# Four transformer layers on one core: layer 2's first maxima from on-chip parts, its router later, and its experts prepared inside the last attention group

## The reference, cut to what matters

```python
# layer 2, x: (1024, 256); xn = layernorm(x); T = 1024, 16 heads, hd = 16
q, k, v = split(xn @ w_qkv.T)
scores = einsum('bhqd,bhkd->bhqk', q, k) * hd ** -0.5      # causal
attn = softmax(scores); attention = (attn @ v) @ w_out.T

scores = xn @ gate_w.T                                      # 8 experts
ew, ei = top_k(scores, 2); ew = softmax(ew)
x1 = silu(einsum('td,ehd->teh', xn, w_gate))
x3 = einsum('td,ehd->teh', xn, w_up)
expert_out = einsum('teh,edh->ted', x1 * x3, w_down)
routed = sum over e of comb[t, e] * expert_out[t, e]        # comb: ew at the chosen experts
shared = (silu(xn @ sh_gate.T) * (xn @ sh_up.T)) @ sh_down.T
x = x + attention + routed + sigmoid(xn @ se_gate_w.T) * shared
```

## Time and profile before

| what | us |
|---|---|
| median of 3 runs (919.77 to 921.51) | 920.62 |
| the profiled execution, as a run | 929.83 |
| its span, first to last instruction | 928.1 |
| TensorE busy in it | 840.9 |
| VectorE, ScalarE, GpSimd busy | 562.2, 386.6, 236.5 |

### The profile page before, as it was taken

One profiled execution on the slowest core, in us unless ns is written; L12 is line 12 of the kernel. 1 busy time (PEld: TensorE's weight loads), 2 busy tenths in 40 slices (PEclk: granted clock), 3 DMA queues, 4 the chain that ended last, 5 costly groups with the idle time before them and its releaser, 6 DMA issues.

```text
span 928.1 us, 12052 instructions
## 1 busy us (share of the span) xinstructions
PE 840.9 (91%) x4835; PEld 497.8 (54%) x4835; DVE 562.2 (61%) x999; ACT 386.6 (42%) x477; POOL 236.5 (25%) x211
## 2 busy tenths in 40 slices
PE   8998999999899999996899998679999889989997
PEld 3554453445354435444478794523333258888776
DVE  3878658774876678216443553577778326964552
ACT  2641345346444645563523402115556763510240
POOL 4641322421142114513321101400111137710110
PEclk8979999999999999998889997769999989999999
DMA  6464069315731850204000004949000061000001
GB/s 187 77 198 124 23 147 162 90 70 86 119 81 68 140 142 1 77 1 152 8 1 1 1 3 152 126 104 121 2 1 1 1 237 47 0 1 1 0 1 46
DMA packets 35584, 64.99 MB, mean 70 GB/s; under 512 B 6164, under 2 KB 14908, under 8 KB 35460
## 3 DMA queue, kind: packets, MB, share of 16 engines
q1 hardware_dynamic: 34952, 64.08, 29.7%
q10 hardware_dynamic: 576, 0.13, 0.1%
HBM read 44.35 MB, written 16.29 MB: 65 GB/s over the span
## 4 chain that ended last, share of the span: by engine, by line
PE 65%; DVE 19%; ACT 5%; DMA 4%; SPq 3%; issue 2%; POOL 2%; ACTq 0%; DVEq 0%; POOLq 0%
PE psD L1808 11%; PE psO L1946 11%; PE psA L1808 10%; PE psD L1891 9%; PE psA L1909 8%; DVE mx L1384 8%; PE psO L1808 7%; PE psA L1908 3%; SPq L604 3%; PE psD L1893 2%; ACT Pr L1054 2%; DVE hid_low L1704 1%; DMA Ks<-in_c_ones4b 1%; PE psD L1960 1%; POOL Pr L905 1%
## 5 line engine op out<-in xcount | busy, mean ns | idle before, releaser
L1384 DVE TENSOR_REDUCE mx<-psD 128x1 f32<-128x512 f32 (+3 forms) x418 | 258.4, 657 | 89.1 <-PE psD L1893 63.7
L1054 ACT ACTIVATE Pr<-psA 128x1024 f32<-128x1024 f32 (+3 forms) x192 | 161.8, 866 | 161.7 <-PE psA L1909 161.3
L905 POOL TENSOR_SCALAR_AFFINE_SELECT Pr<-Pr 128x512 f32<-128x512 f32 x96 | 61.1, 637 | 385.5 <-ACT Pr L1054 309.8
L1059 ACT ACTIVATE Pr<-psA 128x1024 f32<-128x1024 f32 (+3 forms) x96 | 63.6, 703 | 60.6 <-PE psA L1909 60.3
L1946 PE MATMUL psO<-Pr,Vh 128*32 128x512 f32 (+3 forms) x768 | 80.8, 500 | 3.1 <-POOL Pr L905 2.5
L1908 PE MATMUL psA<-Qr,Kr 128*128 128x512 f32 (+3 forms) x192 | 75.0, 404 | 0.7 <-ACT xnT L1014 0.7
L1893 PE MATMUL psD<-maskq,identb 128*128 128x128 bf16 x350 | 70.8, 227 | 0.0
L1909 PE MATMUL psA<-Qr,Kr 113*128 113x512 f32 (+3 forms) x192 | 65.8, 349 | 0.0
L1891 PE MATMUL psD<-Kg,Qs 96*128 96x512 bf16 (+3 forms) x192 | 54.9, 334 | 7.8 <-DVE mx L1384 4.9
L1891 PE MATMUL psD<-Kr,Qr 80*128 80x512 bf16 (+3 forms) x166 | 50.6, 347 | 7.0 <-DVE mx L1384 6.1
L1891 PE MATMUL psD<-Ks,Qs 96*128 96x512 bf16 (+3 forms) x166 | 51.5, 354 | 4.7 <-DVE mx L1384 3.7
(11 more groups left out here) (420 smaller groups left out, 1684.3 us busy)
## 6 DMA issues: line engine op xcount, KB each, us to landing
Qr<-d_qr SPq DMA_DIRECT2D x18, 512.0 KB, 11.6
d_qr<-WB SPq DMA_DIRECT2D x9, 512.0 KB, 3.5
Pr<-d_cb SPq DMA_DIRECT2D x8, 512.0 KB, 7.0
Qs<-d_gq SPq DMA_DIRECT2D x24, 128.0 KB, 4.1
Qs<-d_q SPq DMA_DIRECT2D x24, 128.0 KB
Ks<-d_k SPq DMA_DIRECT2D x24, 128.0 KB
Qr<-d_qn SPq DMA_DIRECT2D x18, 128.0 KB, 7.2
Kr<-d_kn SPq DMA_DIRECT2D x18, 128.0 KB, 7.9
```

Of the source, the lines that this page charges most:

```text
L905: pool.affine_select(out=block_, in_=block_, pattern=[[0, GH], [1, P]], compare_op=ALU.is_ge, fill=0.0, base=0, channel_multiplier=-1).the ...
L1054: act.activation(place[:, h, q0:T], src[:, q0:T], ACT.Exp, scale=score_scale(i)).then_inc(a_drained, 1)
L1059: act.activation(place[:, h:h + 2, q0:T], src[:, :, q0 - HALF:HALF], ACT.Exp, scale=score_scale(i)).then_inc(a_drained, 1)
L1384: dve.tensor_reduce(mx[:, j, part, h0:h0 + nh], src, AX, ALU.max).then_inc(d_drained, 1)
```

## The change

It touches layer 2 alone, in three places.

*The first maxima.* ScalarE now copies each query and key unit twice: the bf16 high part and the fp32 value. VectorE makes four copies of k tile 0's high part, in each of which only the rows of one head are kept (`masked_keys`, with the 0/1 matrix `head`); group 8's maxima are then products of q tile 0's high part with a masked key over all 128 rows, with no stack. k tile 1's product and the values tiles are placed between these units. VectorE splits only u0; GpSimd splits u1, u2 and u3 (three steps each, the first being ScalarE's copy now). SyncE's order is: store u0, store u1, stack 8, store u2, stack 9, store u3, then stacks 10 and 11 (once the first four score units of group 8 are there) and `comb` behind them.

*The router.* Its products come behind (10, 0), the choice of experts at (10, 5), the weights and `magnitudes()` at (11, 1), the weights' transposes and copy at (11, 3). The sigmoid becomes an exponential, an addition and a reciprocal.

*The experts' preparation.* The cuts of the first three pieces (kt 0 to 2) and the high parts of `xnT` (kt 3 and 4) are made by ScalarE inside group 11, with the low parts on GpSimd and VectorE. Behind group 11 expert 0's first product comes at once; the output's transposes follow it, and the transposes of `xn` come before hidden unit 2.

```diff
-                if u < 2:
+                if u == 0:
                     sp.wait_ge(split_done, n)
                 else:
-                    sp.wait_ge(late_split_done, u - 1)
+                    sp.wait_ge(late_split_done, u)
                 load((d_q2, d_k2)[u % 2][:, tile_cols(u // 2), :].rearrange("s d t -> d s t"),
                      split_place(n)[1], split_stored[n % 3])
                 if u == 1:
                     sp.wait_ge(split_stored[0], 16 * 2)
                     sp.wait_ge(split_stored[1], 16 * 2)
                     load_stack(GROUPS[2][0])
+                if u == 2:
                     load_stack(GROUPS[2][1])
             sp.wait_ge(split_stored[0], 16 * 3)
             sp.wait_ge(split_stored[2], 16)
-            sp.wait_ge(a_drained, A["cT"])
-            load(d_cb, seT[:], comb_out)
+            sp.wait_ge(a_filled, A["v2"] + GH)
             load_stack(GROUPS[2][2])
             load_stack(GROUPS[2][3])
+            sp.wait_ge(a_drained, A["cT"])
+            load(d_cb, seT, comb_out)
...
+            for u in (1, 2, 3):
+                pool.wait_ge(a_drained, A["xnT2"] + u + 1)
+                for k in (1, 2, 3):
+                    split_step(3 + u, k, late_split_done)
...
+                    if i == LAST and kt in (1, 2, 3):
+                        piece_low(kt - 1)
...
+                        if (i, kt) == (LAST, 1):
+                            act.wait_ge(se_args, 1)
+                            act.activation(sig3[:], lr[:, 9, 0:3 * NT].rearrange("p (j s) -> p j s", s=3), ACT.Exp,
+                                           scale=-1.0).then_inc(se_ready, 1)
+                        if (i, kt) == (LAST, EXPERTS_KT):
+                            act.wait_ge(split_stored[0], 16 * 3)
+                            copy_units([seT])
...
+                        if i == LAST and kt < 3:
+                            cut_piece(kt)
+                        if i == LAST and 3 <= kt < 3 + DC:
+                            act.activation(x2_high[:, kt - 3, :], xnT[:, kt - 3, :], ACT.Copy).then_inc(x2_cut, 1)
...
-                copy_units([split_place(3 + u)[0]])
+                v, b = split_place(3 + u)
+                src = take()
+                act.activation(b[:, 0], src, ACT.Copy).then_inc(part0_cut, 1)
+                act.activation(v, src, ACT.Copy).then_inc(a_drained, 1)
...
+            act.activation(gam[:, 0:1], ln[:, 1, 0:1], ACT.Exp)
+            act.wait_ge(late_split_done, 3)
+            act.wait_ge(split_stored[0], 16 * 2)
             act.wait_ge(split_stored[1], 16 * 2)
             act.wait_ge(split_stored[2], 16)
             maxima_row(GROUPS[2][0])
...
+            split(3, A["xnT2"] + 1)
+            dve.wait_ge(part0_cut, 2)
+            dve.wait_ge(head_ready, 1)
+            for h in range(GH):
+                dve.tensor_scalar(masked_keys(h), split_place(4)[1][:, 0], head[:, h:h + 1], None,
+                                  ALU.mult).then_inc(keys_masked, 1)
...
+                    pe.wait_ge(keys_masked, GH)
+                    last_keys = None
+                    for k, (j, part, h0, nh, w) in enumerate(MAX_UNITS):
+                        maxima_unit(groups[0], j, h0, nh, w, part)
+                        if k == 3:
+                            last_keys = a_unit()
+                        if k in (3, 8):
+                            features(cols(w_qkv2, 3 * P, 4 * P), normed, halves=(k // 8,), dst=last_keys)
+                        if k >= 13 and k % 3 == 1 and k < 13 + 3 * NT:
+                            value_tile((k - 13) // 3)
+                    maxima_transpose(groups[0], GH)
                     arrived(groups[0])
...
+                        if (i, kt) == LOGITS_AT:
+                            logits = d_unit()
+                            for j in range(NT):
+                                op = product(logits[:, j * (E + 1):(j + 1) * (E + 1)],
+                                             [(xnT[:, k, tile_cols(j)], w_rt2[:, k, :]) for k in range(DC)])
+                            op.then_inc(d_filled, 1)
...
             for m in range(E + DC):
+                if m == 2:
+                    pe.wait_ge(d_drained, DU[f"o{LAST}"])
+                    transposed(xn)
                 pe.wait_ge(piece_split, m + 1)
                 features(weights2(m, 0), parts2, range(3 * DC))
+                if m == 0:
+                    output_transposes(LAST)
+                    pe.wait_ge(gsum_ready, 1)
+                    pe.matmul(d_unit()[:, 0:4], onesf[:], gam[:, 0:4], start=True, stop=True).then_inc(d_filled, 1)
```

More of the change, by code:

```diff
@@ L279, in build @@
         gam = sb("gam", [P, 12])
+        head = sb("head", [P, GH])
         Qr, Kr = over("Qs", "Qr", [P, 8 * T]), over("Ks", "Kr", [P, 8 * T])
@@ L484, in build @@
             + [("xnT1", 1), ("v1a", 1), ("xnT1b", 1), ("qk1", 1), ("v1", 1), ("xh", DC), ("s1", NT), ("gate1", FC)]
-            + [("xnT2", DC), ("qk2", 4), ("v2", 2), ("cT", 1)]
-            + [(f"att{i}", A_GROUP) for i in GROUPS[2]] + [("oT2", DC), ("gate2", E + DC)]
+            + [("xnT2", DC), ("qk2", 4), ("v2", 2)]
+            + [(f"att{i}", A_GROUP) for i in GROUPS[2][:-1]]
+            + [("first of the last", GH * EXPERTS_KT), ("cT", 1), (f"att{LAST}", A_GROUP - GH * EXPERTS_KT)]
+            + [("gate2 first", 2), ("oT2", DC), ("gate2", E + DC - 2)]
             + [("xnT3", DC), ("k3", DC), ("g3", DC), ("sig3", F3C)])
@@ L1477, in attention @@
                 if groups[0] > 0:
-                    magnitudes()
+                    for c in range(DC):
+                        dve.wait_ge(x2_cut, c + 1)
+                        dve.tensor_tensor(x2_low[:, c, :], xnT[:, c, :], x2_high[:, c, :], ALU.subtract).then_inc(x2_split, 1)
                     outputs(groups[-1])
@@ L2049, in attention, with value_tile @@
                     values_product(*behind, (0, 1))
-                    output_transposes(groups[-1])
+            value_place = [None]
+            def value_tile(j):
+                if j % 4 == 0:
+                    value_place[0] = a_unit()
+                op = product(value_place[0][:, (j % 4) * D:(j % 4 + 1) * D],
+                             [(xnT[:, k, tile_cols(j)], w_qkv2[:, k, 2 * D:3 * D]) for k in range(DC)])
+                if j % 4 == 3:
+                    op.then_inc(a_filled, 1)
             def down(u, terms):
```

149 lines of the change are left out of this document (75 added, 74 removed).

## The result

The changed kernel takes 916.77 us (median of 20 runs, 910.76 to 925.68) beside 922.58 us for the kernel before on the same chip (20 runs, 917.92 to 930.27). The ratio is 0.9929, with a 95% interval of 0.9909 to 0.9949: 6.5 us less, 4.7 to 8.4. The prediction was -9.4. By ratio the change is worth less than the two profiles suggest, and the experiments say why.

What follows compares the result with a forecast made beforehand. In layer 2's front nothing computes at the limit; a chain of stores, stack loads and maxima sets it. The terms -12.1 + 0.5 + 3.2 + 2.9 - 3.9 = -9.4 gave 911.2 us, with an 8-in-10 range of 905.5 to 918.5.

Steps and rivals of the forecast that it cites:

- Front, -12.1 and +0.5: Layer 2's front: group 9's first maxima unit at 612.7 instead of 624.8, -12.1; TensorE starting at the low clock, +0.5.
- the wait for stack 9 covers both: Layer 2's front: stack 9, there at 612.7, hides the maxima's end (599 to 604) and first score (602 to 608).
- TensorE waits 5 to 9 us for the last load of a stack just behind the first score: Sign expected in the front's profile after, with group 9's first unit at 612 to 614.
- Masked keys: Layer 2's front: VectorE makes four 128x1024 copies at 0.7 us each, 2.8 us in all, costing nothing behind stack 9's wait.
- Router, +3.2: Group 10, behind kt 0: the 16 small products add 3.2 us, from 2.5 if gaps take some.
- TensorE is nearly always busy in that group, so they are added: Group 10: the reason for counting the router products' 3.2 us in full.
- Last group, +2.9: Group 11: ScalarE gets 4.9 us of cuts, copies and exponential, partly hidden in gaps; +2.9 us, bounds 1.5 and 5.0.
- Experts, -3.9: Start of the experts: expert 0's product follows group 11 at once, 4.3 us come in between; -3.9 us, bounds -5.5 and -2.
- (a): Front: loads move at 353 GB/s or more, maxima set the front; -16.3 in all, 904.3 us; 7 in 100.
- (b): Maxima stage: TensorE's clock stays low, first unit at 622 to 627; -0.6 to +4.4, about 922.5 us; 8 in 100.
- (c): Group 11 and experts: port quarrel slows GpSimd and VectorE, ScalarE's 4.9 us come in full; -1.8, 918.8 us; 13 in 100.
- (d): Front: nothing moves because the new stage waits for something else as late as 624; +2.2 us; 2 in 100.

Runs made afterwards that it cites:

- the second measurement: The changed kernel, unedited, timed and profiled again beside three of its variants: 919.32 us, ratio 0.9966 to the kernel before.

## Why the prediction was right, and where it wasn't

The forecast of faster and the range (905.5 to 918.5) held with 916.77; the narrower 907.5 to 915.5, given 70 in 100, did not, and the second measurement, 919.32, is just outside both. The size was too large. Term by term, from the two profiles on the common clock:

- **Front, -12.1 and +0.5.** Group 9's first unit is at +52.0 instead of +62.9 (608.65 and 624.82, from 556.67 and 561.89), -10.9; up to group 8's `OT` another 0.6 is gained. -11.5 beside a forecast of -11.6. The size is right, but the step "the wait for stack 9 covers both" is wrong. What is late is the row of maxima, which the prediction took at its price in an empty queue and had in time at 602 to 608. The sign "TensorE waits 5 to 9 us for the last load of a stack just behind the first score" failed: the wait is 8.27 us and stands ahead of the score. That the two come out alike is luck. Both end with the queue's traffic, and this ended at 607.0 + 5.2 = 612.2 on the clock of before, where the prediction had stack 9. But the measured traffic has k1's store in it, behind the stack, and the sum had no time for that. The rate rises to a store's, 283 GB/s and more, at 605.0, so stack 9 itself was through near 605, some 2 us earlier than reckoned; the store and the row's late packets filled these 2 us. The prediction had said that it trusted this order least.
- **Masked keys.** 6.2 us for four, where 2.8 was taken. The one that ran without GpSimd took 0.48, less than the 0.7 for one; the others took 1.25 to 2.36 beside GpSimd's split, each ending just behind one of its steps. That is the quarrel of the two engines that the prediction read from the earlier trace rows, and its bounds had allowed for it. In this execution it cost nothing, since the wait for the queue covers it, as the prediction said of all of this stage; where the queue was quick (the row issued at 599.27, the traffic ended at 599.0) the maxima set the front, and these microseconds stand in it. The bound of 577 to 582 for the start of the maxima held (573.70 + 5.2 = 578.9).
- **Router, +3.2: the term that was mis-sized.** It measured +5.1. The products take 3.9 us of it, and the 1.2 left is the clock that falls to half behind them: in the one profile in which it didn't fall, nothing was left. The step "TensorE is nearly always busy in that group, so they are added" counted their length, 0.7 us short, and not the clock behind them. In other executions the same place costs 6.7 us, and up to 8.4 when the later fall of the clock is taken off (38.84 - 1.0 - 29.41). Taking the products out of it gives back 6.5, 7.2 and 7.5 us by three pairs of ratios, each pair from one chip (0.9928 and 0.9858, 0.9949 and 0.9871, 0.9966 and 0.9885; each within 3.4 to 5.7 us, and in the first and the third pair another edit differs too).
- **Last group, +2.9.** It measured +2.5 (23.27 us from `OT` of group 10 to the last values product, 20.81 before). 1.6 of it goes when the preparation is undone; the rest isn't settled.
- **Experts, -3.9.** -3.4 (63.04 us from `OT` of group 11 to the wait at layer 3's end, 66.42 before); a wait of 1.22 us for VectorE stood where 0.9 was taken.
- **Sum.** -11.5 + 5.1 + 2.5 - 3.4 = -7.3, where -9.4 stood. The two profiles differ by 8.9 us on the common clock; the 1.6 us more lie behind the experts, where the change does nothing. The ratios say -6.5 and -3.1. Two places vary enough from one execution to the next to make up such differences, though that they do isn't shown: the router's, 5.1 to 8.4 us, and the front, with its first score at +45.3 to +51.2 for the same program.
- **Rivals.** (a), that the loads are quicker than 131 GB/s, was given 7 in 100. It was not the profile of the changed kernel, but in two of the others the traffic ended by 600.5 and the maxima did set the front, in the quicker one all of it: up to group 8's `OT` 16.4 us were gained. The gain of 16.3 us for the whole still doesn't come, since the router's place costs 6.7 there. (b) fell: the clock was 1.00 from 580 to 600. (c), later groups that take more, came true in part, through the router and not through ports. (d) fell.

What stays open: what holds the row's packets back behind SyncE's traffic; why the same loads move at 168 GB/s in one execution and at 225 in another; why the two halves of stack 9, which end the row's wait, don't show in the time; how the narrow products bring the clock down; and what sets off its later fall.

## What to carry to other kernels

A few very narrow products cost more than their length here, in a stretch that TensorE bounds; in a stretch where TensorE waits for a DMA anyway they cost nothing, as long as the wait is longer than they are. Look for such a wait before choosing the place: here it is worth 6 to 7 us, as much as the whole change. And a small DMA whose result is waited for must be priced with what is in flight when it is issued, on another engine's queue too, and not by its row in an idle queue.

## What the runs showed of the hardware

- A row of 8 KB on ScalarE's queue took 1.8 to 1.9 us from its issue to the score with nothing in flight; its 48 packets were seen 1.2 us after the issue and took 0.2. Behind traffic of SyncE's queue they were seen up to 5.7 us after the issue, and the score came only after that traffic had ended (0.8 to 1.9 us in the table above, 2.1 in the variant with the router's products in the wait), up to 7.74 us after the issue.
- 32 fp32 products of 9 columns took 3.74 us with the clock at full, up to 5.39 where it fell among them. In 8 of 9 profiles 3.4 to 10.3 us at half clock followed or began among them, although TensorE was busy all through those stretches. Eight products of 384 columns among them didn't prevent it.
- A tensor-scalar operation on 128x1024 bf16 took 0.48 us on VectorE while GpSimd was idle. Three more, each beside a step of GpSimd's, took 2.36, 1.25 and 2.34 us, and each ended 0.28 to 0.29 us after that step did. The profile of every variant has the same durations within 0.01 us.
